# Vision tower on one Trainium2 core: mask products added in the attention rounds, the router reordered, the down product with stationary weights

## What is computed

```python
scores = (jnp.einsum('bqhd,bkhd->bhqk', q, k) + mask) * inv_scale
out = jnp.einsum('bhqk,bkhd->bqhd', jax.nn.softmax(scores, axis=-1), v)
h = h + out.reshape(b, s, h * hd)                # layer 1, attention
...
scores = jax.nn.sigmoid(logits)                  # logits = h @ gate_w.T, 32 experts
sc = scores + gate_bias                          # groups of 4 experts
group_scores = jax.lax.top_k(grp, 2)[0].sum(-1)  # 4 of the 8 groups are kept
masked = jnp.where(smask > 0, sc, jnp.zeros_like(sc))
tki = jax.lax.top_k(masked, TOPK)[1]             # then 8 experts of those kept
g = jax.nn.silu(jnp.einsum('th,eih->tei', h, w_gate))
u = jnp.einsum('th,eih->tei', h, w_up)
routed = jnp.einsum('tei,ehi->th', g * u * combine[:, :, None], w_down)
return routed + shared                           # two shared halves, all tokens
```

## Time and profile before

| | |
|---|---|
| time, median of 3 runs | 952.13 us (951.54 to 954.05) |
| time of the profiled execution | 956.0 us |
| its span, first to last instruction | 954.3 us |
| PE busy | 792.1 us (83%) |
| DVE busy | 629.0 us (66%) |
| ACT busy | 410.8 us (43%) |
| POOL busy | 240.5 us (25%) |
| mean granted TensorE clock | 0.889 of full speed |
| chain that ended last | PE 66%, DVE 18%, ACT 6% |

### The profile page before, as it was taken

One profiled execution on the slowest core, in us unless ns is written; L12 is line 12 of the kernel. 1 busy time (PEld: TensorE's weight loads), 2 busy tenths in 40 slices (PEclk: granted clock), 3 DMA queues, 4 the chain that ended last, 5 costly groups with the idle time before them and its releaser, 6 DMA issues.

```text
span 954.3 us, 19243 instructions
## 1 busy us (share of the span) xinstructions
PE 792.1 (83%) x7446; PEld 598.7 (63%) x7446; DVE 629.0 (66%) x922; ACT 410.8 (43%) x590; POOL 240.5 (25%) x218
## 2 busy tenths in 40 slices
PE   2863974998997966877697998589999999999996
PEld 1642743984543554655386885358777777888885
DVE  4584599548876476887767776746777745544454
ACT  6242662540205132766357772445555522222232
POOL 5000399003789811000302330023333300000000
PEclk9985896898999987988899556779999999999999
DMA  7000000020000000010130110024444321222221
GB/s 286 1 1 1 3 1 1 3 90 1 1 0 1 0 2 0 1 36 1 33 74 25 42 48 1 1 91 147 147 145 145 129 64 55 70 66 64 64 64 51
DMA packets 24356, 46.60 MB, mean 49 GB/s; under 512 B 2637, under 2 KB 10573, under 8 KB 23917
## 3 DMA queue, kind: packets, MB, share of 16 engines
q1 hardware_dynamic: 24301, 45.82, 15.4%
HBM read 42.51 MB, written 1.36 MB: 46 GB/s over the span
## 4 chain that ended last, share of the span: by engine, by line
PE 66%; DVE 18%; ACT 6%; issue 6%; POOL 3%; DMA 1%; DVEq 0%; POOLq 0%; ACTq 0%
PE psum L1671 11%; PE psum L1672 11%; PE psum L1673 11%; PE psum L1826 6%; PE psum L1836 4%; PE psum L795 4%; PE psum L796 4%; PE psum L797 4%; PE psum L1954 1%; DVE arena L1359 1%; PE psum L1876 1%; PE psum L1807 1%; ACT arena L1206 1%; DVE arena L1543 1%; DVE hT L1646 1%
## 5 line engine op out<-in xcount | busy, mean ns | idle before, releaser
L1671 PE MATMUL psum<-xh,arena 128*128 128x296 f16 (+1 forms) x664 | 196.2, 296 | 13.6 <-issue 4.9
L1672 PE MATMUL psum<-xl,arena 128*128 128x296 f16 (+1 forms) x664 | 196.3, 296 | 0.0
L1673 PE MATMUL psum<-xh,arena 128*128 128x296 f16 (+1 forms) x664 | 195.9, 295 | 0.0
L795 PE MATMUL psum<-arena 128*128 (+3 forms) x340 | 93.4, 275 | 6.0 <-DVE arena L663 6.0
L718 DVE TENSOR_TENSOR arena<-psum,arena 128x592 f32<-128x592 f32 x64 | 49.6, 775 | 67.9 <-PE psum L1673 58.8
L796 PE MATMUL psum<-arena 128*128 (+3 forms) x340 | 93.5, 275 | 0.0
L797 PE MATMUL psum<-arena 128*128 (+3 forms) x340 | 93.3, 274 | 0.0
L622 ACT ACTIVATE arena<-arena 128x592 f16<-128x592 f32 x68 | 47.4, 697 | 104.6 <-DVE arena L657 104.6
L663 DVE TENSOR_TENSOR arena<-arena 128x592 f16<-128x592 f32 x68 | 52.7, 775 | 59.0 <-ACT arena L622 58.9
L1671 PEld LDWEIGHTS psum<-xh,arena 128*128 (+2 forms) x664 | 66.2, 100 | 35.0 <-issue 15.1
L1671 PE MATMUL psum<-arena 128*74 128x74 f16 (+3 forms) x348 | 59.6, 232 | 30.7 <-POOL arena L917 17.7
(11 more groups left out here) (321 smaller groups left out, 1712.9 us busy)
## 6 DMA issues: line engine op xcount, KB each, us to landing
arena<-comb SPq DMA_DIRECT2D x64, 296.0 KB, 3.3
arena<-in_wmoe SPq DMA_DIRECT2D x34, 384.0 KB, 3.0
arena<-in_xt SPq DMA_DIRECT2D x4, 864.0 KB, 9.1
arena<-in_w SPq DMA_DIRECT2D x2, 1024.0 KB, 6.4
arena<-arena SPq DMA_DIRECT2D x6, 187.0 KB
arena<-in_ctrl SPq DMA_DIRECT2D x1, 1056.0 KB, 9.1
out<-arena SPq DMA_DIRECT2D x2, 512.0 KB, 3.1
arena<-in_wlin SPq DMA_DIRECT2D x1, 768.0 KB, 4.7
```

The lines of the kernel that those rows point to most:

```text
L795: pe.matmul(dst, hi, W[:, i, s_, 0, 2 * D:3 * D], start=start and t % 2 == 0, stop=False, skip_group_check=True)
L1671: pe.matmul(dst, wh, mh, start=start, stop=False)
L1672: pe.matmul(dst, wh, ml, start=False, stop=False)
L1673: return pe.matmul(dst, wl, mh, start=False, stop=stop)
```

## The change

What it does, stage by stage:

- In `mix`, ahead of its products, FILLERS = 4 matmuls write the mask (222 columns each) into columns of the output bank that nobody reads. They come in all 16 rounds. The wait for `att_n` is moved ahead of them.
- LEAD is 4. The high halves are made in rounds 7, 9, 11, 13, the low ones in rounds 9 and 11, and two low ones (`last_lows`) inside the fourth norm, ahead of its reciprocal.
- `turned_back` has 16 instructions of 148 columns without a wait between them.
- TensorE starts the first `gate_up` after two chunks of the norm, and then computes the logits. `hR` and `htok` are gone. The groups are selected by `max` and `match_replace` on 8 scores. The weights of the first two routed experts don't go through DRAM: four matmuls (`first_combine`) spread them over the partitions, and ScalarE copies them.
- The low halves of the other 30 experts are made by VectorE (`weight_low`, the same instruction as L1637), behind the low half of the activations; GpSimd does nothing in this stage, and ScalarE makes no scaled copy.
- `down` has the weights stationary: 12 matmuls of 296 columns, into banks 0, 1, 2 and 7, with features on partitions. The sum is added to `hT`, and `rows_out` transposes it at the end of each half (10 transposes, copied out by ScalarE).

```diff
...
-LEAD = 6
+LEAD = 4
...
-LOW_AT = [3, 5, 7, 9, 11, 13]
+HIGH_AT = [7, 9, 11, 13]
+LOW_AT = [9, 11]
+FILLERS = 4
...
-        router_bank = {("lg",): 7, **{("hR", n): n % 3 for n in range(5)}, **{("cT", n): 7 for n in range(3)}}
+        router_bank = {("lg",): 1, ("cT", 0): 7, ("cT", 1): 0, ("cT", 2): 1}
...
-        GATE_UP, ACC = 3, 0
+        GATE_UP, ACC = 3, (0, 1, 2, 7)
+        SPREAD = (2, 7, 0, 1)
...
-            for s_ in range(2):
-                combine(0, 1, s_)
...
-        def moe_pool(pool):
-            def low(i, s_):
-                return pool.tensor_tensor(W[:, i, s_, 1], wraw[:, s_], W[:, i, s_, 0], ALU.subtract)
...
+        def weight_low(dve, i, s_, count):
+
+            dve.wait_ge(ev["whi"], count)
+            dve.scalar_tensor_tensor(W[:, i, s_, 1], wraw[:, s_], WS, W[:, i, s_, 0], ALU.mult, ALU.subtract).then_inc(
+                ev["wlo"], 1)
...
             act.activation(W[:, i, s_, 0], wraw[:, s_], ACT.Copy, scale=WS).then_inc(ev["whi"], 1)
-            act.activation(wraw[:, s_], wraw[:, s_], ACT.Copy, scale=WS).then_inc(ev["wsc"], 1)
...
+            def first_combine(x):
+                s_, ch = x // 2, x % 2
+                act.wait_ge(ev["spread"], x + 1)
+                ins = act.activation(cb_[:, s_, cols(ch)], banks[SPREAD[x]][:, 0:CH], ACT.Copy)
+                if ch:
...
+            def router():
+                gate(0)
+                full(act, ("lg",))
+                act.activation(scr, bank(("lg",))[:, 0:NT * NE].rearrange("p (i e) -> p i e", e=NE), ACT.Sigmoid).then_inc(emptied["act"], 1)
+                high(0)
+                gate(1)
+                act.wait_ge(ev["al"], 1)
+                act.activation(t1.rearrange("p (c t) -> p c t", c=2), psum[:, GATE_UP + 2:GATE_UP + 4, 0:CH], ACT.Copy,
+                               scale=AS / WS).then_inc(ev["t1"], 1)
+                for x in range(2):
+                    weight_high(act, LEAD // 2, x, 16 * (LEAD // 2 + 1))
+                combine_row(0)
+                high(1)
+                combine_row(1)
+                first_combine(0)
+                first_combine(1)
+                combine_row(2)
+                first_combine(2)
+                first_combine(3)
...
+            shared(0, 0)
...
-            other = gsc.unsqueeze(2).to_broadcast([128, NT, 8, 8])
-            own = gsc.unsqueeze(3).to_broadcast([128, NT, 8, 8])
-            link(dve.tensor_tensor(cmp1, other, own, ALU.is_gt))
...
+            for i in range(NT):
+                link(dve.max(rank[:, i], gsc[:, i]), hold=i == NT - 1)
+            link(dve.tensor_scalar(rank[:, :, 4:8], rank[:, :, 4:8], 0.0, NEG, ALU.mult, ALU.add))
+            rest(0, 0, True)
+            for i in range(NT):
+                link(dve.match_replace(top8[:, i], rank[:, i], gsc[:, i], -NEG), hold=i == NT - 1)
+            link(dve.tensor_scalar(rank, top8, -NEG, None, ALU.is_equal))
...
+            gated(0, 1)
+            weight_low(dve, LEAD // 2, 0, LEAD + 1)
             rest(0, 1, True)
+            weight_low(dve, LEAD // 2, 1, LEAD + 2)
...
+                if hf == 0:
+                    first = (NX - LEAD) // 2
+                    with dve.Fori(1, first) as i:
+                        for s_ in range(2):
+                            turn(i * 2, s_, i * 16)
+                            weight_low(dve, i + LEAD // 2, s_, i * 2 + (LEAD + s_ + 1))
...
+                    tokens = hT[:, c, hf * HALF + CH * ch:hf * HALF + CH * ch + CH]
+                    dve.scalar_tensor_tensor(tokens, psum[:, ACC[x], 0:CH], 1.0 / (AS * WS), tokens, ALU.mult,
+                                             ALU.add).then_inc(ev["summed"], 1)
...
-                for t, _, m in half_tiles(0):
-                    dst = psum[0:m, ACC + t // 2, (t % 2) * D:(t % 2) * D + D]
-                    lo, hi = al[:, s_, 128 * t:128 * t + m], ah[:, s_, 128 * t:128 * t + m]
-
-                    pe.matmul(dst, hi, W[:, i, s_, 0, 2 * D:3 * D], start=start and t % 2 == 0, stop=False, skip_group_check=True)
-                    pe.matmul(dst, hi, W[:, i, s_, 1, 2 * D:3 * D], start=False, stop=False, skip_group_check=True)
...
+                for x in parts:
+                    c, ch = x % 2, x // 2
+                    dst = psum[:, ACC[x], 0:CH]
+                    high, low = (W[:, i, s_, kind, 2 * D + 128 * c:2 * D + 128 * c + 128] for kind in range(2))
+                    pe.matmul(dst, high, ah[:, s_, cols(ch)], start=start, stop=False, skip_group_check=True)
+                    pe.matmul(dst, high, al[:, s_, cols(ch)], start=False, stop=False, skip_group_check=True)
+                    ins = pe.matmul(dst, low, ah[:, s_, cols(ch)], start=False, stop=stop, skip_group_check=True)
...
+            def first_combine():
+                for x in range(4):
+                    s_, ch = x // 2, x % 2
+                    after(pe, ("cT", ch))
+                    if SPREAD[x] == 1:
+                        after(pe, ("cT", 2))
+                    pe.matmul(banks[SPREAD[x]][:, 0:CH], ident[0:32, s_:s_ + 1].to_broadcast([32, 128]),
+                              cT[:, cols(ch)], start=True, stop=True).then_inc(ev["spread"], 1)
+
+            def rows_out(hf):
+                for n in range(3):
+                    pe.wait_ge(ev["summed"], 4 * hf + (2, 4, 4)[n])
+                    for t, _, m in half_tiles(0)[2 * n:2 * n + 2]:
+                        for c in range(2):
+                            at = (t % 2) * D + 128 * c
+                            ins = pe.transpose(banks[ACC[n]][0:m, at:at + 128],
+                                               hT[:, c, hf * HALF + 128 * t:hf * HALF + 128 * t + m], ident[:])
+                    ins.then_inc(ev["outT"], 1)
...
+                if hf == 0:
+                    pe.wait_ge(ev["ln4_xl"], 2)
+                    gate_up(0, 0, 0, 0, True)
+                    logits()
+                    gate_up(0, 0, 1, 0, False)
+                    gate_up(0, 1, 0, 2, False)
+                    combine_rows()
+                    first_combine()
+                    pe.wait_ge(ev["spread_out"], 2)
+                    for s_ in range(2):
+                        pe.wait_ge(ev[f"comb{s_}"], 16)
+                    down(0, 0, 0, start=True)
+                    down(0, 1, 0)
+                    gate_up(0, 1, 1, 2, False)
+                    down(1, 0, 2)
                 else:
-                    after(pe, ("hR", 4))
-                down(hf, 0, 0, base, start=True)
-                if hf == 0:
-                    combine_rows()
-                with pe.Fori(1, NX // 2) as i:
+                    gate_up(hf, 0, 0, base, False)
+                    rows_out(0)
+                    gate_up(hf, 0, 1, base, False)
+                    pe.wait_ge(ev["res"], 3)
+                    down(0, 0, base, start=True)
+                with pe.Fori(1 if hf else 2, NX // 2) as i:
                     gate_up(hf, i, 0, i * 2 + base, False)
-                    down(hf, i - 1, 1, i * 2 + (base - 2))
+                    down(i - 1, 1, i * 2 + (base - 2))
                     gate_up(hf, i, 1, i * 2 + base, False)
-                    down(hf, i, 0, i * 2 + base)
-                down(hf, NX // 2 - 1, 1, base + NX - 2, stop=True)
+                    down(i, 0, i * 2 + base)
+                down(NX // 2 - 1, 1, base + NX - 2, stop=True)
...
-                        for r in range(2):
-                            ins = dve.scalar_tensor_tensor(dst[:, r], src[:, :, 64 * r:64 * r + S], sm("bv", c), dst[:, r],
-                                                       ALU.add, ALU.add)
...
+                        ins = dve.scalar_tensor_tensor(dst, src, sm("bv", c), dst, ALU.add, ALU.add)
...
+            def last_lows():
+                for e in range(len(LOW_AT), LEAD):
+                    weight_low(dve, e // 2, e % 2, e + 1)
+
+            norm("ln4", lead=turned_back, meanwhile=last_lows)
...
+                if k >= 2:
+                    pe.wait_ge(ev["att_n"], k - 1)
+                for _ in range(FILLERS):
+                    pe.matmul(banks[O_BANK + k % 2][0:101, 16 * (DH + 1):16 * (DH + 1) + 6 * S], identb[0:101, 0:101],
+                              causalb[0:101].unsqueeze(1).to_broadcast([101, 6, S]), start=True, stop=True)
                 pe.wait_ge(ev["att_pa"], k + 1)
                 pe.wait_ge(ev["att_pb"], k + 1)
-                if k >= 2:
-                    pe.wait_ge(ev["att_n"], k - 1)
```

172 lines of the change are left out of this document (74 added, 98 removed).

## The result

Measured: before 952.73 us median (951.54 to 954.05), after the change 922.94 us (916.60 to 923.57, 4 runs), a ratio of 0.9672 with a 95% interval of [0.9627, 0.9717]. 921.5 was forecast. The profiled execution took 923.57 us, its span is 921.9.

What follows compares the result with a forecast made beforehand. Bound: TensorE at half clock in attention rounds, at full clock in expert turns, with VectorE's chain adding 0.1 in the first half. Terms -16.7 - 4.5 - 2.5 - 7.9 + 1.0 = -30.6: 956.0 becomes 925.4, median 921.5 us; range 908 to 942.

Steps and rivals of the forecast that it cites:

- A, the stall and the clock: Attention rounds: round 4 starts 4.7 us earlier, TensorE at full clock, 43.8 us against 55.8; -16.7 us.
- B, turning back: Turning back and norm: 16 instructions of about 0.37 us replace 32, late low halves hidden in idle time; -4.5 us.
- C, router: Router: weights ready 2.6 us earlier, VectorE on at about 630, two down products owed; -2.5 us.
- D, turns: Expert turns: 28 at 4.63 us, bound by VectorE, and 4 at 4.54, 147.8 us against 151.6, second half 4.1 less; -7.9.
- E's middle: Ten transposes between the halves cost between 0 and 1.8 us; taken as +0.5 us.
- Rival 3: Turns: the split in VectorE's queue is stretched 2.5 times to 3.5 us, 59 us lost, 980 us; chance 0.03.
- E, ends: Ends of the halves: adds, transposes and a copy at the end +0.5, transposes between the halves +0.5; +1.0 us.
- Rivals 1 and 2: Attention: clock stays low, 946.7 us, chance 0.15; or falls in split rounds and returns late, about 934, chance 0.10.
- rival 2: Attention: clock falls during split rounds 7 to 13 and comes back late, about 934 us; chance 0.10.

Runs made afterwards that it cites:

- the square of four kernels: Start of attention to turning back: before 70.6 us, added products alone 80.0, the rest of the change alone 65.5, both 53.6.
- before_plus_added: The kernel before plus the four added products in each attention round, its early weight splits kept: 962.81 us median, ratio 1.0099.

## Why the prediction was right, point by point

- **A, the stall and the clock** (-16.7, measured -16.6). Right in that both parts of the change are needed; the square of four kernels shows it. From round 4 to the last normalization 43.8 us were worked out; 519.67 to 563.40 are 43.7. That these agree is luck, since sizes inside were off and cancelled. From the start of round 4 to that of round 15 it took 32.8 us, where the terms give 34.3: five passes were 2.84 and three 2.60 (2.75 was taken; the added products cost 0.49, not 0.38), one took 3.80, a split added 0.9 and not 1.40, and a high half alone nothing. From round 15 to the end of the drain it took 11.0, where the terms give 9.6.
- **What made the clock fall before.** The prediction said that it fell when the first low half held VectorE up and TensorE ran out of work, and chose the full clock because "the stall in front of the fall is gone too". The stall is not in front of the fall. In the kernel before, the clock falls in the window from 520.00 to 520.25 us, with TensorE at work; the low half starts at 521.12, and TensorE runs dry from 521.63 to 524.66. Two windows, then the timeline:

```profile
520.00:520.25 0.25, 0.25 (x21) 0.25 (x14) 0.00 (x0) 0.25 (x1) 0.00 (x0) 0.73 0.00 0
520.25:520.50 0.25, 0.25 (x7) 0.22 (x5) 0.00 (x0) 0.25 (x2) 0.06 (x1) 0.50 0.00 0
...
520.35 0.73 PE L1970 MATMUL psum<-arena 101*101 101x296 bf16 x2
...
521.02 0.61 PE L1979 MATMUL psum<-arena 48*64 48x37 f16 x32
521.12 1.40 DVE L1637 SCALAR_TENSOR_TENSOR arena<-arena 128x768 f16<-128x768 f32 x1 [3.40 <-ACT arena L1215]
...
524.66 1.61 PE L1993 MATMUL psum<-identh,arena 101*111 101x101 f16 x15 [3.02 <-DVE arena L1624]
```

  So this stall did not make the clock fall in the kernel before. It would have done so in one with the added products, as before_plus_added shows. The forecast of 1.00 was right; this reason for it was not.
- **The rule on transposes.** "TensorE: Matmul & The Clock Gate" of the Trainium skill, Part 4, says that transposes do not count as busy in the same way for the clock. The prediction read its trace as agreeing so far. The runs here do not bear it out: the kernel with nine transposes in place of four products kept 1.00. Part 1 of that page says that the slow clock is the default and that activity releases it; TensorE at 30.00 us of 30 busy by the profile stayed at 0.50. What in the work of these rounds keeps it there is not shown.
- **B, turning back** (-4.5, measured -6.8). Right in kind, the mis-sized term is L1646's successor: 16 in 4.72 us (2.32 + 2 x 1.20), 0.30 each and not 0.37. Against 10.4 for the 32 before (5.23 + 2 x 2.59) that is 5.7 less. The cover for the late low halves held. Another 0.4 is the shorter wait for TensorE in front (0.66 for 1.03), 0.3 the shorter way from the last square to the reciprocal (2.55 for 2.87), and the last 0.4 lies in small gaps between the instructions.
- **C, router** (-2.5, measured -0.7). Its first half was better than forecast: from the end of the norm to the first L748 are 22.4 us for 29.7, 7.4 less (5.1 by its terms). The logits came 3.3 us later against the end of the norm, where 2 was taken; but from the weights to the first L748 it took 4.3 us (602.46 to 606.71) and before 9.8, where 6.5 was taken for the wait alone. Its second half was worse: from the first to the third are 15.75 for 9.07, 6.7 more where the owed `down` was priced at 3.0. That price is the step that went wrong: TensorE was taken at full clock, and the 24 products, all but the last few at 0.247, took 5.5 us (609.08 to 614.55). They also started only 2.4 us after the first L748, since the last spreading products and their copies came first, at half clock too. The timeline there (L838 spreads, L824 opens `down`):

```profile
602.46 1.29 PE L800 MATMUL psum<-ident,arena 128*32 128x128 f32 x10 [3.92 <-DVE arena L736]
603.75 4.57 PE L838 MATMUL psum<-arena,ident 32*128 32x296 f32 x8
609.08 0.40 PE L824 MATMUL psum<-arena 128*128 128x296 f16 x1 [0.77 <-ACT arena L614]
```

- **D, turns** (-7.9, or -7.4 with E's middle; measured -10.4 with it). In the first half -3.8 became -6.2. "VectorE is the bound there at 4.63" was wrong: the split took 0.96, VectorE's turn in which it does not wait for TensorE is 4.37, and TensorE's 4.54 sets the pace at 4.53. The mis-sized term is again the 1.40 of the earlier trace rows, a duration read beside an engine that has no work there in the changed kernel. Rival 3 stretched the split for that same contention; it went the other way.
- **E, ends** (+1.0). +0.3 at the very end for +0.5; the middle lies in the second half's -4.2 and can't be told apart.
- **Rivals 1 and 2** did not come, but they are near: two products give rival 2's picture (fall at the split rounds), three a late fall. With one product a round less than the change has, the clock was not held to the end.
- **The number.** 921.5 against 922.94 is closer than the terms were. In the traces the change saved 34.2 us from the start of attention on, and 30.6 were forecast: B was 2.3 better, D with E's middle 3.0 and E's end 0.2, C 1.8 and A 0.1 worse. Scatter hid a part of that: attention began 1.8 us later in the trace after, and the repeat of the changed kernel had a ratio of 0.9619 and not 0.9672. The range of 908 to 942 would have held either. B, C and the second half of D rest on the two timelines; no kernel here makes one of these changes alone.

## What to carry to other kernels

When an engine runs at half clock, find the moment of the fall in narrow windows and look at what lies ahead of it: here the long stall lay 1.5 us behind the fall. Then test each cause by itself and with the other: taking the stall out of attention gave 5 us and left the clock low, the added products as well gave 12 more, and the products alone cost 9. Before a duration is carried to another place, ask what ran beside it; VectorE's 1.40 was 0.95 without GpSimd. And compare traces from the first point at which the kernels differ, since 8 us of scatter here lay ahead of it.
